# Keys of both attentions regrouped through DRAM by halves of a chunk instead of by whole chunks

## The reference

```python
x = x + jnp.tanh(g_xattn[0]) * _L0_xattn_ref(_layernorm(x), ctx_1024, ctx_1024, Wq, Wk, Wv, Wo)   # 16 heads of 32
x = x + jnp.tanh(g_ffn[0])   * _L0_ffn_ref(_layernorm(x), w1, conv_w, conv_b, w2)
x = x + jnp.tanh(g_xattn[1]) * _L1_xattn_ref(_layernorm(x), ctx_1024, mask, Wq, Wkv, Wo)          # 8 heads of 64
x = x + jnp.tanh(g_ffn[1])   * _L1_ffn_ref(_layernorm(x), w_gate, w_up, w_down)
```

## Time and profile before

| | us |
|---|---|
| median of 3 runs | 2224.13 |
| lowest, highest | 2219.16, 2231.52 |
| the profiled execution | 2225.15 |
| its span, first to last instruction | 2223.4 |

### The profile page before, as it was taken

One profiled execution on the slowest core, in us unless ns is written; L12 is line 12 of the kernel. 1 busy time (PEld: TensorE's weight loads), 2 busy tenths in 40 slices (PEclk: granted clock), 3 DMA queues, 4 the chain that ended last, 5 costly groups with the idle time before them and its releaser, 6 DMA issues. The chain is left out here.

```text
span 2223.4 us, 42254 instructions
## 1 busy us (share of the span) xinstructions
PE 1949.8 (88%) x15208; PEld 1376.2 (62%) x15208; DVE 1488.3 (67%) x2752; ACT 948.1 (43%) x1289; POOL 1201.5 (54%) x1470
## 2 busy tenths in 40 slices
PE   5798898898897478989678999999999977899997
PEld 3466676676676377777445666666666664455553
DVE  4776776776765479898444666666666546898973
ACT  3276666666667573333132434344344443111111
POOL 4175766766655453232321467577576422787763
PEclk9899999999997589999888999999999988999998
DMA  7454444344330321111163344444444521011100
GB/s 205 103 128 110 103 121 118 103 115 119 101 95 22 126 75 34 41 33 33 53 196 93 92 133 145 126 133 145 136 131 129 178 62 38 24 33 38 33 24 29
DMA packets 184011, 208.67 MB, mean 94 GB/s; under 512 B 61480, under 2 KB 145704, under 8 KB 183336
## 3 DMA queue, kind: packets, MB, share of 16 engines
q1 hardware_dynamic: 183848, 206.46, 32.8%
HBM read 138.61 MB, written 67.53 MB: 93 GB/s over the span
## 5 line engine op out<-in xcount | busy, mean ns | idle before, releaser
L709 POOL TENSOR_TENSOR a_p_hl<-a_p,a_p_hl 125x448 bf16<-125x448 f32 x540 | 564.9, 1048 | 500.9 <-ACT a_p_hl L842 472.7
L1008 DVE TENSOR_REDUCE a_nm<-a_psum 112x1 f32<-112x750 f32 x256 | 237.3, 934 | 127.7 <-PE a_psum L1262 126.2
L832 ACT ACTIVATE a_p<-a_psum 125x1344 f32<-125x1344 f32 x192 | 247.8, 1291 | 149.2 <-PE a_psum L1242 137.9
L842 ACT ACTIVATE a_p_hl<-a_p 125x1344 bf16<-125x1344 f32 x192 | 254.1, 1323 | 97.3 <-PE a_psum L1280 93.3
L1280 PEld LDWEIGHTS a_psum<-a_v_st,a_p_hl 125*128 125x128 bf16 x4608 | 179.9, 99 | 39.4 <-issue 18.9
L1280 PE MATMUL a_psum<-a_v_st,a_p_hl 125*128 125x65 bf16 (+2 forms) x4608 | 191.3, 196 | 10.3 <-POOL a_p_hl L709 4.1
L1913 PE MATMUL f_conv<-f_u,f_taps 128*128 128x224 f32 x768 | 161.3, 360 | 22.3 <-DVE f_u L1765 21.4
L1152 PE MATMUL a_psum<-a_chl,a_w 128*128 128x375 bf16 x768 | 147.2, 339 | 30.9 <-DVE a_w L899 15.5
L1262 PE MATMUL a_psum<-a_k_st,a_q_st 96*112 96x375 bf16 x512 | 131.1, 343 | 42.3 <-DVE a_nm L1008 25.1
L1913 PEld LDWEIGHTS f_conv<-f_u,f_taps 128*128 128x128 f32 x768 | 141.7, 191 | 31.8 <-DVE f_u L1765 27.1
L1152 PE MATMUL a_psum<-a_chl,kept_w 128*128 128x375 bf16 x768 | 137.5, 332 | 23.8 <-DVE kept_w L899 17.9
(11 more groups left out here) (251 smaller groups left out, 4057.8 us busy)
## 6 DMA issues: line engine op xcount, KB each, us to landing
a_k<-a_k_tmp SPq DMA_DIRECT2D x64, 375.0 KB, 3.0
a_k_st<-a_k SPq DMA_DIRECT2D x96, 187.5 KB, 3.3
kept_k<-a_k SPq DMA_DIRECT2D x96, 187.5 KB, 3.4
a_c<-in_ctx_t SPq DMA_DIRECT2D x16, 750.0 KB, 5.8
ctx_parts<-a_chl SPq DMA_DIRECT2D x16, 750.0 KB, 9.6
a_chl<-ctx_parts SPq DMA_DIRECT2D x16, 750.0 KB, 6.1
a_q_st<-a_q SPq DMA_DIRECT2D x192, 56.0 KB, 2.2
rounded<-a_fw SPq DMA_DIRECT2D x24, 352.0 KB, 3.8
```

What stands on the lines that cost most here:

```text
L709: ins = nc.gpsimd.tensor_tensor(p_hl[0:MC, h % 2, 1, cols], p32[0:MC, h % 2, cols], p_hl[0:MC, h % 2, 0, cols], ALU.subtract)
L832: nc.scalar.activation(p32[0:MC, par, :].rearrange("p (b n) -> p b n", b=3), st[0:MC, :, 0:2 * S], ACT.Exp, scale=scale).then_inc(exp_done, 1)
L842: nc.scalar.activation(p_hl[0:MC, par, 0, :], p32[0:MC, par, :], ACT.Copy).then_inc(phi_done, 1)
L1008: ins = nc.vector.tensor_reduce(out, sm_[0:HALF, 0:2, 0:MK], AX.XY, ALU.max, negate=True)
```

## The change

`regroup` gets `half` and `halves`. After *each* half of a chunk of keys it stores that half's 375 columns and reads them into the stacks: two stores and six reads for a chunk of keys, where one and three were. Queries are regrouped as before. A chunk is complete after nine reads. The count for the landed stores is kept in Python, so SP's loop in the first attention is written out too.

```diff
-        N_ST_DMA = 6
+        N_ST_DMA = 9
...
-            pairs = 0 if fp4_weights else PAIRS - 1
+            pairs = 0
...
-            def regroup(b, cc, n_done, sent, tmp, dram, stack, width, parts):
-
+            def regroup(b, cc, n_done, sent, tmp, dram, stack, width, parts, half=0, halves=1):
+
+                cols = slice(half * (width // halves), (half + 1) * (width // halves))
                 sp.wait_ge(unit_done, n_done)
-                sp.dma_start(dram[cc].rearrange("a p n -> p a n"), tmp[:, cc % 2, :, :]).then_inc(sent, 16)
+                sp.dma_start(dram[cc, :, :, cols].rearrange("a p n -> p a n"), tmp[:, cc % 2, :, cols]).then_inc(sent, 16)
                 n_used = value((b.index - 1) * H + (cc + 1) * HC)
-                n_sent = value((b.index * KC + cc + 1) * 16)
+                n_stored[halves] += 16
+                n_sent = n_stored[halves]
...
                     sp.dma_start(stack[row:row + DK, b.parity, c0 * width:(c0 + HC) * width].rearrange(
-                        "p (h n) -> p h n", h=HC), dram[cc, part].rearrange(
+                        "p (h n) -> p h n", h=HC)[:, :, cols], dram[cc, part][:, cols].rearrange(
                         "(h p) n -> p h n", h=HC)).then_inc(st_in[cc], 16)
...
-                if kind == "K" and k[1] == 1:
-                    regroup(b, k[0], value(n), k_sent, k_tmp, k_dram, k_st, M, (0, 1, 0))
+                if kind == "K":
+                    regroup(b, k[0], value(n), k_sent, k_tmp, k_dram, k_st, M, (0, 1, 0), k[1], 2)
...
-                    if step == ("K", (0, 1), b + 1):
+                    if step == ("K", (0, 0), b + 1):
```

More of the change, by code:

```diff
@@ L502, in regroup @@
                     sp.dma_start(stack[row:row + DK, b.parity, c0 * width:(c0 + HC) * width].rearrange(
-                        "p (h n) -> p h n", h=HC), dram[cc, part].rearrange(
+                        "p (h n) -> p h n", h=HC)[:, :, cols], dram[cc, part][:, cols].rearrange(
                         "(h p) n -> p h n", h=HC)).then_inc(st_in[cc], 16)
+            n_stored = {1: 0, 2: 0}
             def move_maxima(b, g, n_done):
```

## The result

The changed kernel takes 2248.87 us (median of 4 runs, 2247.19 to 2250.06) against 2227.41 for the kernel before (4 runs); the ratio is 1.0094, with an interval of 1.0067 to 1.012. The profiled execution took 2249.03 us, its span is 2247.2; PE is busy 87% of it, and SP's DMA queue takes 33.0% of the DMA engines' time, as before. I had predicted 2222, with a range up to 2243, and "no change" as the likeliest.

What follows compares the result with a forecast made beforehand. PE, busy 88%, was taken to bound the kernel. The terms summed to -1, with the first prologue -2.5, against the profiled 2225.15: 2222.6, in terms of the median 2222 us, range 2203 to 2243.

Steps and rivals of the forecast that it cites:

- Both signs of being wrong: Wrong if the first attention does not shorten by 20 to 30 us, or the second not lengthen by 15 to 35.
- Part 1: First attention, quarter 0: shorter store behind K(0,1) brings Q0's stack 2.0 us earlier in six rows, -12 us.
- Part 2: First attention: the load of the context's second half comes earlier, shortening ACT's and PE's waits, -8 us.
- Part 3: First attention: shorter quarter-0 waits spare four of the clock drops of 1.7 us, -7 us.
- The 1.5 us that the first prologue was to give: First attention's prologue: about 1.5 us gained by the same shortened chain of stores and reads.
- Part 4: Second attention, quarter 0: K(0,1)'s reads end 1.85 us later behind K(0,0)'s regrouping, in six rows, +11 us.
- Part 5: Second attention: K(1,0)'s regrouping delays the piece of weights, DVE waits 4 to 5 us, PE 1 a row, +6 us.
- Part 6: Second attention: prologue's unhidden stores +7 us; first row's queries' wait and clock -5; clock drops in four more rows +7.
- Case B: Rival: the second attention's queue prevails, delaying keys and weights, total 2241 or 2246 us; chance 0.20.
- main case: First attention's gain and second attention's loss cancel: 2222 us, own range 2213 to 2234; chance 0.50.
- case A: Rival: the first attention's gain prevails, as half reads land earlier and rows have slack, 2206 us; chance 0.27.
- estimate of the prediction from its table: From the skill's DMA table: a 187.5 KB shorter store is only 1.0 us shorter, the rest paid twice.

Runs made afterwards that it cites:

- run 1: The changed kernel with halves in the first attention alone, all the second attention's keys regrouped whole: 2204.27 us, ratio 0.991.
- run 7: The changed kernel with halves only in the first attention's rows; its prologue and all of the second attention whole: 2204.98 us, ratio 0.9916.
- run 10: The changed kernel with the second attention's halves kept only for chunk 0 in the rows; its other chunks and prologue whole: 2234.04 us, ratio 1.0044.
- run 11: The changed kernel with the second attention's halves kept only for chunk 1 in the rows; its other chunks and prologue whole: 2217.70 us, ratio 0.9983.
- run 5: The changed kernel with the second attention's chunk 1 of the keys regrouped whole from row 2 on: 2245.02 us, ratio 1.0096.
- run 6: The changed kernel with the second attention's halves kept only for chunks 2 and 3 in the rows; chunks 0, 1 and prologue whole: 2204.23 us, ratio 0.9916.

## Why the prediction was wrong

The mechanisms were those of the prediction. The sizes were off on both sides: the gains smaller, the losses larger. Since the sum was a small difference of large terms, that decided its sign. Both signs of being wrong that the prediction named came: the first attention became 15.3 us shorter by its end (18.8 from its row 0, quarter 1, on) and not 20 to 30, the second 37 longer and not 15 to 35. Step by step:

**Part 1, stacks of the first attention: -12, measured -8.1.** The working for the row shown was right (store 2.37 for 2.35, Q0's 2.15 for 1.95). Wrong was to take it six times: the rows gained 1.8, 1.2, 1.2, 1.4, 1.6 and 0.9. In rows 5 and 7 Q0's store still takes 3.6 and 3.7 us, and PE waits 2.31 (3.72 and 3.19 before). What makes that store slow there was not tried.

**Part 2, the context: -8, measured -4.3 in PE's wait.** ACT's wait went nearly to nothing, as forecast (8.9 to 1.1 us behind the start). But five of PE's six waits now stop at 1.4 us: behind the load comes DVE's own order of work, which I had named ("not all arrives") and priced too low.

**Part 3, the clock: -7, measured -3.4 in this trace and -6.8 in run 1's.** The stretch 184 to 191 went from 0.76 to 1.00. Between quarter 3 of row 0 and quarter 3 of row 7 the clock cost 10.2 us before, 6.8 here and 3.4 in run 1. In the first 180 us the clock fell from 0.94 to 0.91, some 5 us; why is open. The 1.5 us that the first prologue was to give had the wrong sign: it costs 0.6 here and 4.3 in run 1 (run 7 has the reason). Run 1, with its 18 us, says that parts 1 to 3 are together nearer to 18 than to 28.

**Part 4, quarter 0 of the second attention: +11, measured +18.2 in PE's waits for `kept_k`.** This is the step that failed most: the added time of SP's queue per row, put at 1.85 us, is 3.9. I worked it out at one row and took it six times, and that row was the exception. Its whole store took 3.89 us to the reads, the slowest of the six (the others 3.30, 2.78, 2.85, 3.10, 3.46, mean of all 3.23), and the half I had put at 2.35 takes 2.77 in the mean of the twelve of the changed kernel (2.37 to 3.29). So halving saves 0.46 of a store and not 1.5, and each row has nearly a whole regrouping more: from Q0's store to the end of the keys' reads SP takes 10.64, 10.48, 9.52, 9.67, 9.85, 11.41 us before and 12.96, 15.25, 13.33, 13.76, 14.12, 15.74 after, which is 2.3 more in the row that I had worked out (1.85 forecast) and 4.3 in the mean of the other five. There is a second reason that the trace before shows: in the row worked out SP is free and K(0,0) ready 0.9 us before K(0,1), so that the first half gets ahead by as much, while in rows 3, 6 and 7 SP is done with Q0's reads 0.1 us or less before it sends the keys, and the first half gets no start. With the half's store still put at 2.35, the six rows give 1.8, 3.3, 2.8, 2.9, 3.4 and 3.1, an estimate of 17 in place of 11. The rest is the store of a half. Run 10 has the price of this step with its clock: 30 us.

**Part 5, what stands behind: +6, measured +3.8 in PE's waits for Q1's stack, and hidden.** The load was late and DVE waited, 1.8 us a row and not 4 to 5. Alone it costs 13 (run 11), behind part 4's delay 4 (run 5).

**Part 6: prologue +7, measured +11.4; first row -5, measured -5.1 up to its quarter 1; clock +7, measured +10 (from quarter 2 of row 1 to quarter 3 of row 7 it cost 3.4 us before and 13.7 after).** In the prologue I counted three chunks; SP's queue goes from regrouping to regrouping from 1116.86 until the context's read at 1169.15, and four chunks stand ahead of that. One queries' store there took 3.14 before and 2.30 after, so it fell by 0.8 and not by 1.45; 3.7 - 0.8 is 2.9 for each of four. The upper bound of 19 had held it.

**The rivals.** Case B, "the second attention's queue prevails", is what happened, at 2241 to 2246 in the forecast and 2249 measured, with its chance of 0.20. Of its own condition, 2.2 us a row more than the main case, about 1.0 could have been read from the trace before, as worked out under part 4: the six stores of chunk 0 stand there, and five are shorter than the one I took.

Two readings that spoke for case A were wrong. The row at 1448.58 waited 0.27 us, and I took that for a reserve. But a row that waits at all has none: its wait grew to 2.99. And the window at 1263.10 to 1265.10 with its 334 GB/s holds no reads of the keys. The queue had sent those by 1251.85, and what moved there is the second of two reads of the context:

```profile
1256.92 4.61 SPq L429 DMA_DIRECT2D a_chl<-ctx_parts  x2
```

The Trainium skill's rule ("DMA: Bandwidth & Descriptors", Bandwidth: batch DMAs) pointed the right way for the second attention, for a reason that no bandwidth shows: run 6 has the same small pieces at no cost. The estimate of the prediction from its table, a half's store 1.0 us shorter, was too large as well: it is 0.46 here. What is paid twice is the wait of SP for the landing (2.8 us) and the issue of three reads (1.9), and it costs only where something that is waited for is queued behind it.

## What to carry to other kernels

Splitting a transfer with a wait in the middle (store, landing, read back) shortened the path here where the first piece had idle time in its queue ahead of the second; where both pieces were ready before the queue came to them, the split added 4.3 to 4.8 us to everything behind. So change such a helper place by place, not in the helper: here the first attention gains 18 us, and three places of the second lose 45 together. And when a step is costed at one row and multiplied, look at the same store in all the rows first.

## What the runs showed of the hardware

Halving 375 KB (median 3.0 us to landing) to 187.5 KB gives 2.6, and reads of 187.5 KB (3.3 and 3.4) become 2.4 and 2.6 at 93.8 KB: with half the bytes, 0.73 to 0.87 of the time. The issue of a read of `kept_k` takes 0.6 us at either size. The same store right behind a 448 KB load took 5.1 to 5.6 to its reads, in six rows. A longer wait of PE cost more than itself: chunk 0 in halves made PE wait 15.4 us more for keys (22.5 in run 10 against 7.1 in run 1), and the kernel 30 us longer. Most of the rest is the clock at its lower level behind those waits: it cost 17.1 us in run 10 and 3.4 in run 1, from quarter 2 of row 1 to quarter 3 of row 7. The kernel before alone spread from 2212 to 2236 us over 29 runs, wider than in the first three.
